# Two bias loads moved to ScalarE's queue, and a narrower wait ahead of the weight transposes

## What is computed

```
qp = ctx @ Wq.T + bq ;  kp = ctx @ Wk.T + bk            (128 wide)
scores = (qp @ kp.T) / sqrt(128) * layernorm(x)         (512 x 512, per batch)
x = x + softmax(where(mask, -inf, scores))
xn = layernorm(x)
x = x + shared_ffn(xn) + sum of the two chosen experts' ffn(xn), each of 8
```

## Time and profile before

| | us |
|---|---|
| median of three runs | 427.13 |
| lowest, highest | 426.73, 428.84 |
| the profiled execution | 426.92 |
| its span, first to last record | 425.2 |
| PE busy | 361.2 (85%) |
| DVE busy | 229.1 (54%) |
| POOL busy | 223.9 (53%) |
| ACT busy | 179.0 (42%) |

### The profile page before, as it was taken

The page is one execution under the profiler, slowest core; times in us unless marked ns, Lnnn a source line. Parts: engine busy times, 40 slices in busy tenths (PEclk is TensorE's granted clock), DMA queues, the critical chain, the costliest instruction groups (busy, mean ns, idle before and its releaser), DMA issues.

```text
span 425.2 us, 7338 instructions
## 1 busy us (share of the span) xinstructions
PE 361.2 (85%) x1582; PEld 234.3 (55%) x1583; DVE 229.1 (54%) x466; ACT 179.0 (42%) x386; POOL 223.9 (53%) x230
## 2 busy tenths in 40 slices
PE   1776677788798889799989899999999999999991
PEld 1333455578464459466656556566565555656550
DVE  3468978984557987756533434444444343434341
ACT  2455535352565442657533333343434333434430
POOL 3369798986063470449154444444544444444422
PEclk9968755655698999989998999999999999999997
DMA  7835979797846444878243555555555555554545
GB/s 244 264 104 193 321 240 304 239 305 261 309 154 216 151 150 149 272 242 274 79 72 78 98 99 99 99 99 99 99 90 102 94 95 90 95 106 77 96 81 65
DMA packets 37303, 67.00 MB, mean 158 GB/s; under 512 B 4832, under 2 KB 8672, under 8 KB 37280
## 3 DMA queue, kind: packets, MB, share of 16 engines
q1 hardware_dynamic: 27600, 44.72, 31.4%
q0 software_dynamic: 9008, 21.50, 27.5%
q10 hardware_dynamic: 672, 0.52, 0.4%
HBM read 38.68 MB, written 28.05 MB: 157 GB/s over the span
## 4 chain that ended last, share of the span: by engine, by line
PE 53%; DMA 13%; DVE 11%; issue 11%; ACT 5%; POOL 2%; POOLq 1%; SPq 1%; ACTq 0%; DVEq 0%
PE bank L1125 9%; DMA sc<-xn_rows,jgather 8%; PE bank L1132 8%; PE bank L1139 8%; PE bank L1051 5%; PE bank L1173 4%; PE bank L1167 4%; PE bank L1170 3%; DMA out_rows<-xin,jscatter 3%; PE bank L1113 3%; PE bank L1157 3%; PE bank L1044 2%; PE bank L1060 2%; ACT bank L603 2%; PE bank L1204 2%
## 5 line engine op out<-in xcount | busy, mean ns | idle before, releaser
L547 POOL DMA_INDIRECT out_rows<-xin,jscatter x39 | 62.0, 1590 | 106.6 <-DMA out_rows<-xin,jscatter 58.3
L964 DVE SCALAR_TENSOR_TENSOR h<-bank,jprob,h 128x256 f32<-128x256 f32 x55 | 26.5, 482 | 103.8 <-ACT h L680 103.8
L680 ACT ACTIVATE h<-bank,jprob 128x256 f32<-128x256 f32 x55 | 26.1, 475 | 113.7 <-PE bank L1132 84.6
L1125 PE MATMUL bank<-gu_hi,x_hi 128*128 x220 | 68.3, 434 | 2.0 <-ACT x_hi L662 2.0
L1139 PE MATMUL bank<-gu_hi,x_lo 128*128 x220 | 63.5, 411 | 0.0
L1132 PE MATMUL bank<-gu_lo,x_bf 128*128 x220 | 59.3, 394 | 0.0
L1173 PE MATMUL bank<-dn_hi,h_lo 128*128 x110 | 44.8, 488 | 6.8 <-DVE h_lo L941 6.8
L525 POOL DMA_INDIRECT sc<-xn_rows,jgather x39 | 43.2, 1108 | 13.8 <-issue 13.7
L1139 PEld LDWEIGHTS bank<-gu_hi,x_lo 128*128 128x128 f32 x220 | 42.4, 193 | 10.9 <-issue 0.5
L456 POOL TENSOR_TENSOR gu_lo<-stage,gu_hi 128x512 bf16<-128x512 f32 (+1 forms) x18 | 23.1, 1281 | 42.2 <-ACT gu_hi L616 42.2
L1125 PEld LDWEIGHTS bank<-gu_hi,x_hi 128*128 128x128 f32 x220 | 39.5, 197 | 10.4 <-issue 3.2
(11 more groups left out here) (130 smaller groups left out, 580.4 us busy)
## 6 DMA issues: line engine op xcount, KB each, us to landing
stage<-in_L_ffn_gate_up_w SPq DMA_DIRECT2D x32, 256.0 KB
xin<-in_x SPq DMA_DIRECT2D x16, 256.0 KB, 4.1
out_rows<-x SPq DMA_DIRECT2D x16, 256.0 KB, 3.2
xn_rows<-xn SPq DMA_DIRECT2D x16, 256.0 KB, 2.6
xn_transposed<-xT SPq DMA_DIRECT2D x16, 256.0 KB, 2.7
stage<-in_L_ffn_down_w SPq DMA_DIRECT2D x16, 256.0 KB, 4.4
sc<-xn_transposed SPq DMA_DIRECT2D x16, 256.0 KB, 2.7
x<-out_rows SPq DMA_DIRECT2D x16, 256.0 KB, 3.1
```

The costliest lines, as they stand in the source:

```text
L547: g.indirect_dma_start(out=out, out_offset=bass.IndirectOffsetOnAxis(ap=jscatter[:, n - TILES:n - TILES + 1], axis=0), in_=y[:, r, :], in_ ...
L1125: tn.matmul(ps_g[r % 2][:], x_hi[:, r % 2, k, :], gu_hi[:, e, k, :], start=(k == 0), stop=False)
```

## The change

The two bias loads leave SP's list. ACT issues them ahead of the two mask loads, and they count on a semaphore of their own, `ld_bias`. PE's wait ahead of the weight transposes goes from 64 to 32. ACT's wait for the biases, the scaling of `bq` and the wait for its result move from the head of ACT's stream to a place behind the copy of the first batch's transposed context, ahead of the first projections.

```diff
-        ld_ctx0 = sem("ld_ctx0")
+        ld_ctx0, ld_bias = sem("ld_ctx0"), sem("ld_bias")
...
             sp.dma_start(wqk[:, 0, :], wq).then_inc(ld_small, 16)
             sp.dma_start(wqk[:, 1, :], wk).then_inc(ld_small, 16)
             sp.dma_start(ctx_in[:, 0:RT], ctx_rows[:, 0:RT]).then_inc(ld_ctx0, 16)
-            sp.dma_start(bqk[:, 0:1], bq.rearrange("(p o) -> p o", o=1)).then_inc(ld_small, 16)
-            sp.dma_start(bqk[:, 1:2], bk.rearrange("(p o) -> p o", o=1)).then_inc(ld_small, 16)
             sp.dma_start(xin[:, 0, :], x_t[0]).then_inc(ld_x[0], 16)
...
         def _(act):
             a = nc.scalar
+            act.dma_start(bqk[:, 0:1], bq.rearrange("(p o) -> p o", o=1)).then_inc(ld_bias, 16)
+            act.dma_start(bqk[:, 1:2], bk.rearrange("(p o) -> p o", o=1)).then_inc(ld_bias, 16)
             act.dma_start(mask_in[:], mask.rearrange("(r p) s -> p r s", p=P)).then_inc(ld_mask, 16)
...
-            act.wait_ge(ld_small, 64)
-            a.mul(bqk[:, 0:1], bqk[:, 0:1], SCALING).then_inc(bq_ready, 1)
             act.wait_ge(wT_ps, 1)
             a.copy(wqkT[:].rearrange("p w o -> p (w o)"), ps_proj[0][:, 0:2 * H]).then_inc(wT_ready, 1)
-            act.wait_ge(bq_ready, 1)
...
             ctx_copy(0)
+            act.wait_ge(ld_bias, 32)
+            a.mul(bqk[:, 0:1], bqk[:, 0:1], SCALING).then_inc(bq_ready, 1)
+            act.wait_ge(bq_ready, 1)
             projections(0)
...
             pe.wait_ge(c_pool, 1)
-            pe.wait_ge(ld_small, 64)
+            pe.wait_ge(ld_small, 32)
```

## The result

The first comparison gave a median of 423.08 us (420.81 to 427.38, four runs) against 427.75 us (426.73 to 428.84, four runs), a ratio of 0.9872 with an interval of 0.9823 to 0.9921. The forecast was 426.3 us with a range from 424.6 to 428.2, so the time lay outside. The ratios in this document count only the runs within 1.5% of their kernel's fastest; medians, and differences of medians, count all.

The account below looks back on a forecast made before the run. The prediction took the opening's wait for `bk`'s landing as the bound, the first context close behind. A gain of 0.8 us at the first scores, carried to the end, gave span 424.4, profiled 426.1, median 426.3 us; range 424.6 to 428.2.

Parts of the forecast that it names:

- What bounds the kernel: Opening: everything stands on `bk`'s landing at 7.65 us, the first context's at 7.24 next; narrower wait gains 0.88 us there.
- When the first context lands: Opening loads: landing taken as unchanged at 7.24 us, bounds 6.31 and 7.65; moving the loads gives nothing here.
- The next bound: Rest of the context, ahead of first scores: lands some tenths earlier, caps the gain at 0.73 us or more; 0.8 taken.
- the zeros as a danger for the first context: Rival, opening: POOL's 1 MB write delays the first context, up to 10 us; total 427.5 to 429.0 us, chance 0.07.
- ACT's queue: Mask loads issued about 1.0 us later; delay of 0 to 2 us covered by 4.6 us of slack, nothing on the path.
- The scaling of `bq`: Behind ACT's copy of the context: its 0.20 us runs while PE projects and costs nothing.
- Behind the opening: After the first scores: the 0.8 us gain is carried to the end, except for what PE's clock makes of it.
- the better side: Rival, attention stage: clock steps fall favourably, one pair of projections 1.8 us shorter, total 424.5 us; chance 0.12.
- the clock rises no earlier: Rival, first scores: run partly at the lower clock, costing up to 0.6 of the 0.8 us, total 426.9; chance 0.13.
- over 2 would show it wrong: Sign, first score to end: distance stays 410.1 us; a difference above 2 us makes the prediction wrong.
- The spread: Whole kernel: three runs of the same program differ by 2.1 us, about 0.5%, taken as what a measurement can tell.

Follow-up runs that it names:

- e2: The kernel before with only PE's narrower wait, the biases left in SP's list behind the first context: median 423.1 us against 426.0, ratio 0.9953.
- e4: The changed kernel with POOL's write of zeros issued only after the rest of the context landed, ACT's wait for it moved: 424.6 us, kernel before 426.0.
- e7: The kernel before, unedited, run again against itself for a second trace: median 427.2 us against 427.1, ratio 1.016.
- f2: The kernel before with only the narrower wait, plus 15 identity transposes behind the second pair of projections: median 424.9 us, kernel before 427.3.
- f1: The kernel before plus 15 identity transposes in PE's idle time behind the second pair of projections: median 424.0 us against 427.3, ratio 0.9951.
- l6: The kernel before plus six unused identity transposes in each attention step: 441.0 us against 428.5, a single run.
- l12: The kernel before plus twelve unused identity transposes in each attention step: 439.2 us against 428.5, a single run.

## Why the prediction was wrong, point by point

**What bounds the kernel** was right: `bk` was the last of the small loads, and the first context the next. The mechanism as worked out is that of e2 from the landing of the context on, to 0.2 us: context transposes at 7.52 (7.37 worked out), first scores at 14.40 (14.33).

**When the first context lands** is the first step that failed. I took 7.24 us and gave bounds of 6.31 and 7.65; it landed at 5.5, and at 5.8, 6.1 and 6.5 in the other traces of the changed kernel. The argument that neither the load nor what shares the engines with it changes in sum overlooked which transfers run first: the masks, which had taken 58% of the engines' time from 2 to 3 us, now came later. The lower bound was taken from a load in the same queue, which stood behind the same masks.

**The next bound** had the wrong sign. I expected the rest of the context some tenths earlier; it landed 0.75 us later, in company with the zeros. From 6 to 8 us the masks' queue, now later, held 88 and 76% of the engines, and from 10 to 12 us the zeros held 88%; I had seen the zeros as a danger for the first context and the masks only. With the zeros late (e4) it landed at 11.9. So 2.7 us at the projections became 0.63 at the scores, where I had put 0.8: the right size by two errors. (The other traces scatter by as much: the scores start at 15.1 and 15.9 us in before and at 14.5 to 15.0 in the changed kernel.)

**ACT's queue.** The masks' delay was put between 0 and 2 us; it was 2.8 (8.65 against 5.85). That was outside the estimate, and the slack of 4.6 us still covered it: POOL's first penalty was ready at 12.90 + 1.13 = 14.0, and its reader started at 16.97. In e4, whose scores are early, it no longer does.

**The scaling of `bq`** ran at 7.18 us, beside PE's start, at no cost, as forecast.

**Behind the opening** is the step that made the prediction wrong: "except for what PE's clock makes of it" was left out of the sum, and it is nearly the whole result. I had read the fall of the clock in the earlier trace rows, with its price of 1.8 us for a pair of projections, and the idle time of 1.94 us in the same row, and treated it as chance, with 0.12 for the better side. It is chance only in part. In the changed kernel PE waits 2.83 us for a load at 11 to 14 us, its clock falls at 14.8 rather than at 21.1, and the second scores and projections, which nobody waits for, run slowly and fill the time until DVE is ready. The idle time is 0.96 us in all four traces of it instead of 1.94, and the clock stays up when the third projections come, on which much waits. All four have this, both traces of before have the opposite. In the first of the four the slow stretch put the third tile's scores off by about 0.1 us, since DVE's result was there only at 20.50. The prediction's price for this, 1.8 us, counted the pair of projections alone; the scores (1.71 against 1.12) and the four transposes (1.06 against 0.60) make it 2.85. The rival "the clock rises no earlier" had the right matmuls, the first scores, but neither the reason (the clock fell at 14.8 behind a wait, it didn't rise late) nor the sign of the result. Its price of 0.6 us was misread too: the score of 1.71 us at 20.74 ran partly at the upper level, as the fall came at 21.1, and one wholly at the lower level took 2.08 us (e7 at 29.19).

From the first scores to the end it took 422.3 - 14.50 = 407.8 us instead of 410.1, 2.3 us less; the text said that over 2 would show it wrong.

**The spread.** I took 2.1 us between three runs for the noise. Over the runs of before, without the three far ones, it is 14 us (418.4 to 432.4), and a median of four is uncertain by more than the effect. The true difference, 2.4 us, would have been in the range if taken from the median of 427.13.

What stays open: why e2's clock did not fall. One trace had 1.93 us of idle time without a fall, four others with 1.93 to 2.69 us had it, and none of the nine with 0.97 us or less. The Trainium skill, in "TensorE: Matmul & The Clock Gate", section "What's actually happening", says that the monitor runs freely and isn't reset at a kernel's start. By that rule the same idle time would let the clock fall in some executions only; no trace shows one program both ways. If e2 were such a program, f2 should have gained on it, which its runs don't show. Nor does one fall, worth under 3 us, account for a spread of 14 us between timed runs, which the traces don't explain. That the stage is shorter because the clock stays up at this one place is shown by the traces, one execution of each program; that the difference of the medians comes from it too rests on f1's twelve runs and isn't shown for the timed runs one by one.

## What to carry to other kernels

When two loads change queue, look at what they push back, not only at what they free: the big transfers behind them decide what lands when on shared engines. And when a change moves PE's work in a stage with idle times of about 2 us, price a fall of the clock at each idle time as a term of the sum, with a chance; a slow stretch where nobody waits can be cheaper than a fast one that ends in an idle time. Before believing 1% from four runs, compare the kernel with itself.

## What the runs showed of the hardware that I had not expected

Two 0.5 KB loads, 4 bytes for each partition, issued first, landed in 2.3 and 2.4 us and took 13.7% of the engines' time in the microsecond that held 264 packets. The clock's fall behind an idle time of 1.94 us, 3.78 us instead of 1.98 for a pair of projections, could be taken away with 15 transposes of 0.12 us each. The same transposes in every step (l6, l12) made the kernel 11 to 13 us slower, so here filling paid only where PE would otherwise wait.
